# A decoder layer on one core: linear attention in chunks of 64 tokens instead of 128

## What is computed

```python
def step(kv, qkv):                      # one chunk of CHUNK = 128 tokens
    qi, ki, vi = qkv
    inter = jnp.einsum('bhcd,bhde->bhce', qi * q_decay[None, :, :, None], kv)
    scores = jnp.einsum('bhcd,bhsd->bhcs', qi, ki) * dmask[None]
    intra = jnp.einsum('bhcs,bhse->bhce', scores, vi)
    kv_new = r_C[None, :, None, None] * kv + jnp.einsum('bhcd,bhce->bhde', ki * k_decay[None, :, :, None], vi)
    return (kv_new, inter + intra)
...
x = x + attention(layernorm(x))         # RMS norm and Wo after the heads
x = x + softmax(layernorm(sim))         # sim: x against the context, softmax over 256 keys
x = x + experts(layernorm(x))           # top 2 of 8 experts, weighted by a softmax over the two
```

## Time and profile before

| what | value |
|---|---|
| median of 3 runs | 180.23 us (179.91 to 180.83) |
| span of the profiled execution | 178.7 us |
| PE busy | 152.3 us (85%) |
| weight loads (PEld) busy | 106.6 us (60%) |
| DVE busy | 126.4 us (71%) |
| ACT busy | 61.8 us (35%) |
| POOL busy | 35.9 us (20%) |

### The profile page before, as it was taken

The page is one execution under the profiler, slowest core; times in us unless marked ns, Lnnn a source line. Parts: engine busy times, 40 slices in busy tenths (PEclk is TensorE's granted clock), DMA queues, the critical chain, the costliest instruction groups (busy, mean ns, idle before and its releaser), DMA issues.

```text
span 178.7 us, 3036 instructions
## 1 busy us (share of the span) xinstructions
PE 152.3 (85%) x983; PEld 106.6 (60%) x983; DVE 126.4 (71%) x396; ACT 61.8 (35%) x171; POOL 35.9 (20%) x54
## 2 busy tenths in 40 slices
PE   0399964797997999999959999999599889998991
PEld 0267433573662678867626888677258757745880
DVE  0633599647487995975789959757899565877762
ACT  3346880103487132054751320547613220311110
POOL 3104163013161002222410013125100113010020
PEclk9999996569999999999999999999999999999999
DMA  5999200000200000000004000000010000001001
GB/s 173 290 360 340 57 0 4 0 0 2 69 10 0 0 4 0 0 2 0 0 4 132 0 0 0 0 0 0 0 59 0 4 2 0 0 0 59 4 0 59
DMA packets 7930, 7.29 MB, mean 41 GB/s; under 512 B 2264, under 2 KB 7664, under 8 KB 7792
## 3 DMA queue, kind: packets, MB, share of 16 engines
q1 hardware_dynamic: 7424, 6.79, 12.1%
q10 hardware_dynamic: 496, 0.37, 0.7%
HBM read 6.11 MB, written 1.05 MB: 40 GB/s over the span
## 4 chain that ended last, share of the span: by engine, by line
PE 43%; DVE 33%; issue 7%; ACT 6%; DVEq 5%; POOL 3%; DMA 2%; POOLq 0%
PE bank L784 15%; PE ebank L784 11%; DVE probs L613 9%; PE bank L894 4%; POOL rs L325 3%; DVE b_e_parts L738 3%; DVE stats L519 2%; ACT qx L425 2%; PE ebank L792 2%; DMA xin<-in_x 2%; DVE norm L530 2%; DVEq L520 2%; PE bank L799 2%; DVE acc L557 2%; PE bank L890 1%
## 5 line engine op out<-in xcount | busy, mean ns | idle before, releaser
L613 DVE TENSOR_TENSOR probs<-bank,dec 128x512 f32<-128x512 f32 x32 | 19.8, 683 | 1.9 <-PE bank L852 1.9
L852 PE MATMUL bank<-qx,kT 64*128 64x512 f32 x64 | 18.4, 625 | 0.7 <-ACT kv L480 0.7
L325 POOL TENSOR_TENSOR rs<-ve,nhalf 128x2 f32<-128x2 f32 x16 | 11.4, 711 | 36.6 <-DVE ve L524 36.5
L877 PE MATMUL bank<-probs,vpad 128*32 128x128 f32 x256 | 10.8, 293 | 4.1 <-DVE probs L613 4.1
L799 PE MATMUL bank<-cst,norm 128*128 128x128 f32 x36 | 6.4, 301 | 9.1 <-DVE norm L530 9.1
L784 PE MATMUL ebank<-w_e_hi,h3T_hi 128*128 128x512 f32 x40 | 13.3, 413 | 0.0
L557 DVE SCALAR_TENSOR_TENSOR acc<-ebank,gate,acc 128x256 f32<-128x256 f32 x26 | 11.3, 477 | 2.5 <-PE ebank L784 2.3
L425 ACT ACTIVATE qx<-bank,cst 128x256 f32<-128x256 f32 x32 | 12.6, 489 | 0.0
L557 DVE SCALAR_TENSOR_TENSOR acc<-bank,gate,acc 128x256 f32<-128x256 f32 x22 | 9.3, 478 | 4.5 <-PE bank L784 3.0
L784 PE MATMUL ebank<-w_e_hi,h3T_lo 128*128 128x512 f32 x40 | 12.5, 393 | 0.0
L784 PE MATMUL ebank<-w_e_lo,h3T_hi 128*128 128x512 f32 x40 | 12.4, 392 | 0.0
(11 more groups left out here) (135 smaller groups left out, 332.8 us busy)
## 6 DMA issues: line engine op xcount, KB each, us to landing
w_e<-in_L_ffn_We SPq DMA_DIRECT2D x2, 1024.0 KB, 10.8
xin<-in_x SPq DMA_DIRECT2D x4, 256.0 KB, 3.6
dec<-in_decay SPq DMA_DIRECT2D x1, 1024.0 KB, 7.9
out<-outb SPq DMA_DIRECT2D x8, 128.0 KB, 1.7
cst<-in_consts ACTq DMA_DIRECT2D x1, 282.0 KB, 3.6
w_qkv<-in_L_attn_Wq SPq DMA_DIRECT2D x1, 256.0 KB, 4.2
w_qkv<-in_L_attn_Wk SPq DMA_DIRECT2D x1, 256.0 KB, 4.6
w_qkv<-in_L_attn_Wv SPq DMA_DIRECT2D x1, 256.0 KB, 4.9
```

The costliest lines, as they stand in the source:

```text
L325: nc.gpsimd.tensor_tensor(dst[:], src[:], nhalf[:], ALU.pow).then_inc(done, 1)
L613: nc.vector.tensor_tensor(probs[:, t, 4 * n:4 * n + 4, :], bank[2 + n][:].rearrange("p (h n) -> p h n", h=4), dec[:, 4 * n:4 * n + 4, :], ...
L852: pe.matmul(bank[2 + n][:], kT[rows, t, g, :], qx[rows, t, g, :, :], start=True, stop=True).then_inc(s_sc_ps, 1)
L877: mm = pe.matmul(bank[t][32 * q:32 * q + 32, g * P:(g + 1) * P], vpad[:, t, h, :], probs[:, t, h, :], start=(par == 0), stop=(par == 1 and ...
```

## The change

The two tiles of 128 tokens become four chunks of 64. Per batch and tile it does this:

- `qx` holds two masked copies of q instead of four. `scores(t)` forms 16 products (32 rows, 64 by 128) instead of 4 (64 rows, 128 by 512); the four row groups write into four banks, and one semaphore step at the end of the tile replaces four.
- `decay_scores(t)` reads two banks at once, 2 instructions instead of 4 of the same size. The decay table is half as large.
- POOL forms `kd` in four versions instead of one. `state_product` forms three states of 32x32 blocks with 32 products of 32 columns instead of 2 of 128, and stands behind `scores(1)`. DVE's masking of them stands behind `decay_scores(1)`.
- `qd` is written in three instructions of 64 tokens each, for the chunks that have a past.
- `attend()` is one function for both tiles: 64 products of 64 rows and 64 columns for the scores and 24 of 32 rows for the states, instead of 32 and 8 of 128 rows and 128 columns. It waits for all `probs` and the states, and releases ACT once at its end.
- The transposes of the gates wait for ACT's copies of the attention, since they write bank 0.
- The hardware loop over i = 2, 3 is written out. `keep_clock`, which feeds PE with filler matmuls, issues twice as many of half the width.

```diff
@@ -255,12 +261,12 @@
 
         block = stack.enter_context(nc.Block())
 
-        def passes(eng, body):
+        def passes(body):
 
 
             body(0, True, False, False)
             body(1, True, True, False)
-            with eng.Fori(2, B) as i:
+            for i in range(2, B):
                 body(i, True, True, True)
...
@@ -347,10 +353,16 @@
                                                 ALU.mult).then_inc(s_rb, 1)
                 if front:
 
+                    kdec = cst[:, C_KDEC:C_QDEC].rearrange("p (v h) -> p v h", v=STATES)
                     pool.wait_ge(s_rot, TILES * i + 1)
-                    kdec = cst[:, C_KDEC:C_KDEC + H].unsqueeze(2).to_broadcast([P, H, DH])
-                    nc.gpsimd.tensor_tensor(kd[:].rearrange("p (h d) -> p h d", h=H),
-                                            qk[:, 0, D:].rearrange("p (h d) -> p h d", h=H), kdec,
+                    for v in range(STATES):
+                        nc.gpsimd.tensor_tensor(kd[:, v].rearrange("p (h d) -> p h d", h=H),
+                                                qk[:, 0, D:].rearrange("p (h d) -> p h d", h=H),
+                                                kdec[:, v].unsqueeze(2).to_broadcast([P, H, DH]), ALU.mult)
+                    pool.wait_ge(s_rot, TILES * i + 2)
+                    nc.gpsimd.tensor_tensor(kd[:, STATES].rearrange("p (h d) -> p h d", h=H),
+                                            qk[:, 1, D:].rearrange("p (h d) -> p h d", h=H),
+                                            kdec[:, 0].unsqueeze(2).to_broadcast([P, H, DH]),
                                             ALU.mult).then_inc(s_kd, 1)
                 if back:
                     rsqrt(rs[2], ve[2], i - 1, s_var[2], s_rstd[2])
...
@@ -421,17 +433,17 @@
 
                     act.wait_ge(s_qkT_ps, TILES * i + t + 1)
                     act.copy(kT[:, t], bank[t][:, D:].rearrange("p (g n) -> p g n", g=GROUPS))
-                    for k in range(4):
+                    for k in range(2):
                         o = act.activation(qx[:, t, :, k, :], bank[t][:, 0:D].rearrange("p (g n) -> p g n", g=GROUPS),
                                            ACT.Copy, scale=cst[:, C_PICK + k:C_PICK + k + 1])
                     o.then_inc(s_qkT, 1)
 
                 def attention_out(t):
 
-                    act.wait_ge(s_at_ps, TILES * i + t + 1)
-                    src = bank[t][:, 0:D].rearrange("p (g n) -> p g n", g=GROUPS)
-                    act.activation(sqT[:, t], src, ACT.Square)
-                    act.copy(attT[:, t], src).then_inc(s_at, 1)
+                    act.wait_ge(s_at_ps, i + 1)
+                    src = banks[:, 0:HALVES, 0:D].rearrange("p c (t g n) -> p t g c n", t=TILES, g=GROUPS)[:, t]
+                    act.activation(sqT[:, t].rearrange("p g (c n) -> p g c n", c=HALVES), src, ACT.Square)
+                    act.copy(attT[:, t].rearrange("p g (c n) -> p g c n", c=HALVES), src).then_inc(s_at, 1)
 
                 if back:
                     transposed(1, j, bank[4:6], pT)
...
@@ -608,11 +620,22 @@
 
                 def decay_scores(t):
 
-                    for n in range(QUADS):
-                        dve.wait_ge(s_sc_ps, QUADS * (TILES * i + t) + n + 1)
-                        nc.vector.tensor_tensor(probs[:, t, 4 * n:4 * n + 4, :],
-                                                bank[2 + n][:].rearrange("p (h n) -> p h n", h=4),
-                                                dec[:, 4 * n:4 * n + 4, :], ALU.mult).then_inc(s_sc, 1)
+                    dve.wait_ge(s_sc_ps, TILES * i + t + 1)
+                    for n in range(2):
+                        two = slice(2 * n, 2 * n + 2)
+                        nc.vector.tensor_tensor(probs[:, t, two], banks[:, 2 + 2 * n:4 + 2 * n, 0:GROUPS * 2 * CH],
+                                                dec[:, two], ALU.mult).then_inc(s_sc, 1)
+
+                def decay_queries(t):
+
+                    dve.wait_ge(s_qkT, TILES * i + t + 1)
+                    at = CH if t == 0 else 0
+                    qdec = cst[:, C_QDEC:C_PICK].rearrange("p (g n) -> p g n", g=GROUPS)
+                    src = bank[t][:, 0:D].rearrange("p (g n) -> p g n", g=GROUPS)
+                    for h in range(t ^ 1, HALVES):
+                        cols = slice(h * CH, (h + 1) * CH)
+                        o = nc.vector.tensor_tensor(qd[:, t, :, cols], src[:, :, cols], qdec, ALU.mult)
+                    o.then_inc(s_qd, 1)
 
                 def route():
 
@@ -718,20 +741,12 @@
                         dve.wait_ge(s_dec, 16)
                     decay_scores(0)
 
-                    dve.wait_ge(s_qkT, TILES * i + 2)
                     if back:
-                        dve.wait_ge(s_at_ps, TILES * i)
-                    nc.vector.tensor_tensor(qd[:], bank[1][:, 0:D].rearrange("p (g n) -> p g n", g=GROUPS),
-                                            cst[:, C_QDEC:C_QDEC + D].rearrange("p (g n) -> p g n", g=GROUPS),
-                                            ALU.mult).then_inc(s_qd, 1)
+                        dve.wait_ge(s_at_ps, i)
+                    decay_queries(0)
+                    decay_queries(1)
                 if back:
                     low_parts(2, j, ln3_banks, h3T)
-                if front:
-
-                    dve.wait_ge(s_st_ps, i + 1)
-                    nc.vector.tensor_tensor(state[:], bank[0][:, 0:D].rearrange("p (g n) -> p g n", g=GROUPS),
-                                            cst[:, C_BLOCK:C_BLOCK + P].unsqueeze(1).to_broadcast([P, GROUPS, P]),
-                                            ALU.mult).then_inc(s_st, 1)
                 if front and not back:
 
                     dve.wait_ge(s_be_hi, 1)
@@ -740,6 +755,10 @@
                     nc.vector.tensor_tensor(w_r_s[:, :, 1, :], w_r[:], w_r_s[:, :, 0, :].bitcast(F32), ALU.subtract).then_inc(s_lo, 1)
                 if front:
                     decay_scores(1)
+                    dve.wait_ge(s_st_ps, i + 1)
+                    block = cst[:, C_BLOCK:C_IOTA].unsqueeze(1).to_broadcast([P, STATES * GROUPS, 2 * DH])
+                    nc.vector.tensor_tensor(state[:], bank[0][:, 0:STATES * GROUPS * 2 * DH].rearrange(
+                        "p (k n) -> p k n", n=2 * DH), block, ALU.mult).then_inc(s_st, 1)
                 if back:
                     route()
                 if front and not back:
...
@@ -788,8 +807,8 @@
             def keep_clock(n, dst):
 
 
-                for _ in range(n):
-                    pe.matmul(dst[:], ident, cst[:, 0:512], start=True, stop=True)
+                for _ in range(2 * n):
+                    pe.matmul(dst[:, 0:256], ident, cst[:, 0:256], start=True, stop=True)
 
             def transposes(n, b, banks):
 
@@ -843,44 +862,57 @@
 
                     pe.wait_ge(s_v, TILES * (i + 1))
                     pe.wait_ge(s_qkT, TILES * i + t + 1)
+                    if t > 0:
+                        pe.wait_ge(s_sc, 2 * (TILES * i + t))
                     for g in range(GROUPS):
-                        for half in range(2):
-                            n = 2 * g + half
-                            if t > 0:
-                                pe.wait_ge(s_sc, QUADS * (TILES * i + t - 1) + n + 1)
-                            rows = slice(64 * half, 64 * half + 64)
-                            pe.matmul(bank[2 + n][:], kT[rows, t, g, :], qx[rows, t, g, :, :],
-                                      start=True, stop=True).then_inc(s_sc_ps, 1)
+                        for c in range(HALVES):
+                            half = slice(c * CH, (c + 1) * CH)
+                            for r in range(PAIRS):
+                                rows = slice(32 * r, 32 * r + 32)
+                                mm = pe.matmul(bank[2 + r][half, g * P:(g + 1) * P], kT[rows, t, g, half],
+                                               qx[rows, t, g, :, half], start=True, stop=True)
+                    mm.then_inc(s_sc_ps, 1)
 
                 def state_product():
 
                     pe.wait_ge(s_kd, i + 1)
-                    for g in range(GROUPS):
-                        vg = vpad[:, 0].rearrange("p (k a) n -> p k (a n)", a=2)[:, g * PAIRS:(g + 1) * PAIRS]
-                        vg = vg.rearrange("p k (u n) -> p k u n", n=DH)[:, :, 0:4:3, :]
-                        mm = pe.matmul(bank[0][:, g * P:(g + 1) * P], kd[:, g * P:(g + 1) * P], vg,
-                                       start=True, stop=True)
+                    pe.wait_ge(s_qd, TILES * (i + 1))
+                    for t, v, n in ((0, 0, 0), (0, 1, 1), (0, 2, 2), (1, STATES, 2)):
+                        for g in range(GROUPS):
+                            for q in range(PAIRS):
+                                pair = vpad[:, t].rearrange("p (k a) n -> p k (a n)", a=2)[:, g * PAIRS + q]
+                                pair = pair.rearrange("p (u n) -> p u n", n=DH)[:, 0:4:3, :]
+                                at = (n * GROUPS + g) * 2 * DH
```

(52 more changed lines are left out.)

56 lines of the change are left out of this document (31 added, 25 removed).

## The result

The changed kernel is slower. The median is 189.14 us (185.42 to 192.35) against 180.5 us (179.91 to 180.83) for the kernel before on the same chip: 1.0316 times its time, 95% interval 1.0255 to 1.0378. The forecast was 175.6 us, with 182.5 as its upper bound.

A forecast was written before the change was run, and what follows sets the result against it. DVE was taken to set the attention stretch's pace until PE or ACT is late; 178.7 - 4.4 (first batch) - 0.3 (three later batches) = 174.0 span, plus 1.5 for the median: 175.6 us, own range 173.5 to 178, whole range to 182.5.

The forecast's parts named there:

- The first batch: First batch: the projections start at 30.3 instead of 33.86, -3.6 us, and with the clock's -0.8 together -4.4.
- The race: First batch: DVE's b_e_parts runs 0.3 us before POOL's L360, so its 4.62 us aren't paid; losing it had 22%.
- attend(), called hidden: First batch: attend(), from 24.1 to 26.6, lies under DVE's wait for POOL and costs nothing.
- the 0.8 us for it: First batch's projections: about 1.7 of their 5.2 us is the half clock's; half of that counted as gained, -0.8.
- DVE's terms: Later attention stretches: `probs` done at 1.29 us instead of 2.48, three `qd` 0.6 us, `state` done at 4.1.
- PE's terms: Later attention stretches: scores 0.65 us plus 0.1 and 0.27, state product 0.6, attend() 2.5 (bounds 2.1 and 4.8).
- Rival C: Small passes start no faster than 0.027 us each; attend() 4.7 us, +11.4 over three batches, about 187; chance 12%.
- D: In attend(), the four diagonal state blocks wait for each other: 2.5 us instead of 0.64, 181.3 in all; chance 8%.
- The 0.2 us for a change of tiling: attend() on PE: 0.2 us added for a change of tiling, within its 2.5 us.
- the wait predicted: ACT's `gexp` queues behind attention_out(0), which waits for all of attend(); `gden` at 7.6 us against 7.52 before.
- The step that failed: PE's clock falls between scores(0) and scores(1): +2 us per fall, 180 to 182; chance 13% for two or three.
- the forecast's +0.1 a batch: Later attention stretches: DVE's 1.9 us gain is lost waiting for `gexp`, leaving +0.1 us per batch before -0.2 from other edits.

The follow-up runs named there:

- a_fill: The changed kernel plus four filler products of 256 columns on PE behind scores(0): 187.28 us, ratio 1.0323.
- a_hold: `a_fill` with six fillers instead of four in the third and fourth batch, and one more wide product between the transposes and scores(1): 189.25 us, no ratio.
- m_stream: The kernel before, unrolled, with four streams of 128 small products (256 passes) at its end, wide fillers between: first stream 4.88 us.
- a_gap: `a_hold` with all its products plus two wide filler products between tile 0 and tile 1 of attend(): 187.6 us, ratio 1.0388.

## Why the prediction was wrong

**The first batch: the mechanism right, its size half.** The race was won by the step given for it; `b_e_parts` started at 22.78 (22.3 predicted). The projections started at 31.30, not 30.3. That DVE's `w_e_lo` has to wait for POOL was right: it ended 2.14 us after POOL, at 30.17 instead of 29.67, because POOL itself started at 23.50 and not at 22.94. The rest is attend(), called hidden: with its pauses and half the clock it lasted until 30.5, and ACT's two copies behind it made the last wait. The clock was lost, so the 0.8 us for it didn't come, and the gain was 2.27 us instead of 4.4.

**DVE's terms: right.** `probs` 1.28 us a tile (1.29), three `qd` 0.68 (0.6), second `probs` 2.68 us after the first (2.55), `state` done at 4.2 (4.1).

**PE's terms: right in size, at full clock and with instructions at hand.** Scores 0.70 us (1.02 with first load and last pass), state product 0.76 (0.6) in `a_fill`. attend() was predicted at 2.5 us; the fourth batch of `a_hold` needs 2.9, 0.5 of it idle. Rival C, that small passes start no faster than 27 ns, is refuted as a mechanism by 10.7 ns in `m_stream`, and so is, between products on different parts of the array, the floor of about 25 ns that the Trainium skill, TensorE: Matmul & The Clock Gate, section "Wait — 56ns, not 53.3ns?", states. D is refuted too: the 24 products on the diagonal take 0.87 us for 48 passes (`a_gap`, above), not 2.5. The 0.2 us for a change of tiling in the sum of attend() stands in no row and no run measured it.

**`gexp`: the wait predicted, not its length.** It is `gden`'s releaser, as said, but 10.15 us after `probs` instead of 7.6. The last sum of the prediction, 174.0 and 1.5, gives 175.5 and not 175.6, which changes nothing.

**The step that failed** is the one that gave the clock one sentence: "nearer the first. A fall doubles some 3.4 us of attention work, of which DVE hides about 1.5: +2 each, 180 to 182", with a chance of 13%. Its condition was met in every later batch: between scores(0) and scores(1) PE was busy for 0.76 us of 3.67, 1.08 of 4.39 and 0.92 of 4.39. The row that I weighed spoke for it (a clock of 0.51 after a stretch of 0.56 us busy in 3.4), and the last 3 us before `probs`, 0.94 us busy, lay nearer to that than to 1.87. Its size was wrong as well. I ended the fall with attend(), but it lasts through the projections and gate transposes to the first experts (57 to 70.7), and all PE work in it doubles while DVE, through its part by 62.8, hides nothing more. So each batch lost 3.0 to 5.5 us and not 2.

**What no rival had** is the supply of instructions. I priced attend()'s 176 passes by how fast the array can start them, not by how fast they arrive. In the changed kernel itself it shows in the first batch and once more for 0.34 us in the fourth, since at half clock the passes are slow enough for the packets to be there; that is why it hides behind the clock, and why each filler that mended the clock met it. Where both are nearly absent (`a_hold`'s fourth batch) the stretch takes 11.38 us, against 11.12 by my sum. So the forecast's +0.1 a batch was a sum for a state that no batch of the changed kernel was in.

Why the pause is 1.8 us in one batch of `a_hold` and 0.5 in another with the same instructions is answered in part: the packet starts 0.95 us after attend()'s first product in the second batch and 0.85 before it in the fourth. What decides when a packet starts stays open; a kernel with its code shifted was not run. Nor is it settled how the 10.8 us of the profiled execution would divide if the clock alone were held.

## What to carry to other kernels

Halving PE's score products was worth less than nothing here, since PE then idled: ask what the granted clock does in the emptier stretch, and price a fall with everything that PE runs until it is dense again, not only with the stage itself. Count instructions as well as columns: a run of 256 short passes cost 19 to 22 ns each here, whatever the array could do, so what helps is fewer of them, and wide work among them is in part free. Look for the instruction packets beside an idle that no semaphore explains. And where two engines race with 0.7 us between them, write the order down with a semaphore; edits elsewhere moved the winner.

## What the runs showed of the hardware

- PE starts passes of 64 columns on 16 array positions of 32x32 every 10.7 ns, on 8 of 64x32 every 10.8, on 4 of 128x32 every 15.1, until it stands for 2.07, 2.39 and 1.10 us with no semaphore to wait for.
- Such idles end 1.24 to 1.57 us after a 16 KB packet of instructions has landed on queue 8 (31 of 31). From the packet's start to PE's next product it is 2.25 to 2.90 us, and two packets go with 256 passes and their weight loads.
- Issuing each score product twice took a kernel from 1.016 to 0.988 times the time of before; the mean granted clock of the executions behind these ratios went from 0.932 to 0.941 up to 0.979 and 0.99.
- While POOL runs its 4.5 us subtraction of two SBUF tensors, a DVE subtraction of two SBUF tensors that starts later isn't done before it. The 32x256 `b_e_parts` (0.42 us alone) ends 0.27 or 0.28 us after POOL in all six kernels where they meet, and shows as 3.04 to 4.62 us; the 128x2048 `w_e_lo` (2.20 us alone) ends 2.14 or 2.15 us after POOL in all ten, and shows as 3.61 to 4.94.
